# Identity products on TensorE in its waits between the stages of an eight-layer transformer kernel

## The chip, the cores and the metric

The kernel runs on one core of one Trainium2 chip. The metric is the device time in microseconds of one execution. TensorE is called PE here, VectorE DVE, ScalarE ACT and GpSimd POOL.

## What is computed

Tokens x of shape (8, 256, 128) pass four times through an attention and a feed-forward layer, each with a residual and ahead of each a layer norm without gain; a context of shape (8, 64, 128) feeds the attention layers. Cut to the order:

```python
x = x + L0_xattn(layernorm(x), ctx)          # 16 heads, one key/value head
x = x + L0_ffn(layernorm(x))                 # soft mixture: 16 experts, 64 slots each, gelu
x = x + L1_xattn(layernorm(x), ctx)          # similarity w1.q + w2.c + w3.(q*c), both directions
x = x + L1_ffn(layernorm(x))                 # 64 experts of width 88, top 8, two shared experts
x = x + L2_xattn(layernorm(x), ctx, ctx)
x = x + L2_ffn(layernorm(x))                 # 8 experts (4x128, 4x256), top 2, relu squared
x = x + L3_xattn(ctx, ctx, layernorm(x))
x = x + L3_ffn(layernorm(x))                 # quantised linear, depthwise convolution, silu, linear
```

The routed experts are computed for all tokens, and a token's weight for an expert (zero where it isn't chosen) multiplies the hidden values.

## The kernel before

The 2048 tokens lie in SBUF as 16 tiles of 128; four tiles make a group g (512 columns when transposed), so each layer has four groups. The layers are numbered 0 to 7 in the code (L, two to each pair above). Each engine has its own program, written out by hand, and they meet only by semaphores; an engine's order of work is the order of its lines.

At the border of two layers the same chain runs for each group: the residual is added on DVE (L1233, or L1391, L1433, L1581 and L1642 behind attention), DVE takes mean and variance (L1189, L1192, L1195), POOL the inverse root (L586), and DVE (L1202) or POOL (L591, L592) makes xn. On PE ln_transpose waits for xn (semaphore ln_xn), and transposes four tiles with the identity (L1729); ACT copies the result to SBUF (L762). ln_transposes(L) does the four groups one after the other; layers 3 and 5 have router products between them.

Behind the expert stage of layer 1 (eo, comb_ready) PE multiplies the context with w_sim2, then waits for cw_done (DVE L1398), transposes layer 2's groups and makes similarities. The waits for sim_sub and e1_norm stand ahead of transposes at L1968 and L1972. Layer 3 begins with its router products and the shared experts (shared_gate_up); then PE waits for sil_s, and chunk_group1(0, True) begins the 44 chunks of the routed experts with a wait for the first weights' low part (wgu_lo, POOL L624), which POOL makes only when the routing weights are ready (DVE L1480). Inside it, routing_rows transposes them and spreads them over the partitions. After the experts come layer 4 (project, scores, and an attention output per tile t that waits for x_done), layer 5 (router, combine_rows2, 12 chunks of experts), layer 6 in the form of layer 4, and layer 7.

mm is the helper at L1710 that issues every product that isn't a transpose; transposes have their own lines. A product of fp32 operands shows as two MATMUL instructions in the trace, one of fp32r operands as one. psum is eight banks of 512 columns; bank(k) is one of them.

Of the kernel before, what the change touches and what calls it, by code (L numbers as in the profile page):

```python
# [12 lines left out]
P = 128  # L13
# [34 lines left out]
def build_program(nc, A, out):  # L48
    with ExitStack() as ctx:
        def sb(name, shape, dt=F32):  # L50
            return ctx.enter_context(nc.sbuf_tensor(name, shape, dt))
# [4 lines left out]
        psum = ctx.enter_context(nc.psum_tensor("psum", [P, 8, 512], F32))  # L56
# [6 lines left out]
        ident = sb("ident", [P, P])  # L63
# [76 lines left out]
        def bank(k):  # L140
            return psum[:, k, :]
# [1566 lines left out]
        def _(pe):  # L1708
            def mm(dst, lhsT, rhs, start=True, stop=True):
                return pe.matmul(dst, lhsT=lhsT, rhs=rhs, start=start, stop=stop)  # L1710

            def product(dst, w, x):
# [2 lines left out]
                mm(dst, w(0), x(1), False, False)  # L1715
                return mm(dst, w(1), x(0), False, True)

            def ln_transpose(L, g):
                pe.wait_ge(ln_xn, NG * L + g + 1)
                into = LN_BANKS[L][g] if L in LN_BANKS else 6 + g % 2  # L1720
                if g >= 2 and L not in LN_BANKS:
                    pe.wait_ge(ln_xnT, NG * L + g - 1)
                if g == 1 and L == 1:
                    pe.wait_ge(x_done, NT)
                if L == 3 and g == 3:
                    pe.wait_ge(ln_xnT, NG * L + 1)
                    pe.wait_ge(xh_lo, 1 + E0)
                for j in range(4):
                    last = pe.transpose(psum[:, into, P * j:P * j + P], xn[:, 4 * g + j, :], ident[:, :])  # L1729
                last.then_inc(ln_tp, 1)  # L1730

            def ln_transposes(L):
                for g in range(NG):
                    ln_transpose(L, g)
# [15 lines left out]
            for t in range(NT + 3):  # L1750
# [18 lines left out]
                if t >= 3:  # L1769
                    u = t - 3  # L1770
# [4 lines left out]
                if 1 <= t <= NT:  # L1775
                    u = t - 1
# [5 lines left out]
                if t >= 3:  # L1782
                    u = t - 3
# [4 lines left out]
                if 2 <= t <= NT + 1:  # L1788
                    u = t - 2
# [11 lines left out]
            for g in range(NG - 1):  # L1801
                ln_transpose(1, g)
# [55 lines left out]
            pe.wait_ge(se_T, 2)  # L1858
            logits_slots(0)
            ln_transpose(1, NG - 1)  # L1860
            logits_slots(1)
            for q in range(4 * B + 2):
# [76 lines left out]
            for q in range(B // 2):  # L1939
                last = mm(psum[:, 0, q:q + 1], ctxT[:, P * q:P * q + P], cols[:, COL["w_sim2"]:COL["w_sim2"] + 1])  # L1940
            last.then_inc(simT_mm, 1)

            def sim_T(q):

                pe.wait_ge(simT_sb, q + 2)
                for a in range(TB):
                    last = pe.transpose(psum[:, 4 + q // 2, 256 * (q % 2) + P * a:256 * (q % 2) + P * a + P],
                                        simT[:, q, P * a:P * a + P], ident[:, :])
                if q % 2:
                    last.then_inc(sim_mm, 1)  # L1950

            pe.wait_ge(cw_done, 1)
            for q in range(B // 2 + 2):
# [9 lines left out]
                if q >= 2:  # L1963
                    sim_T(q - 2)

            pe.wait_ge(sim_sub, 2)
            for a in range(TB):
                last = pe.transpose(psum[0:B, 7, P * a:P * a + P], mx1b[:, B * a:B * a + B], ident[:, :])  # L1968
            last.then_inc(bt_tp, 1)
            for u in range(NT // 2):  # L1970
                pe.wait_ge(e1_norm, u // 4 + 1)
                last = pe.transpose(psum[:, 2 + u // 4, P * (u % 4):P * (u % 4) + P],  # L1972
                                    e1n[:, 2 * u:2 * u + 2, :].rearrange("p r j -> p (r j)"), ident[:, :])
                if u % 4 == 3:
                    last.then_inc(aT_tp, 1)
# [57 lines left out]
            def gate_up1(n, s, slot):  # L2033

                q, k = s % 4, s % 2
                if later(n, 2):
                    pe.wait_ge(nl_done, n - 1)
                product(bank(k), lambda h: wgu[:, slot, h, 0:P], lambda h: norm_half(q, h)).then_inc(gate_ready, 1)
                if later(n, 2):
                    pe.wait_ge(hid_done, n - 1)  # L2040
                product(bank(2 + k), lambda h: wgu[:, slot, h, P:2 * P], lambda h: norm_half(q, h)).then_inc(up_ready, 1)

            def down1(n, s, slot, start=False, stop=False):
                pe.wait_ge(hh_lo, n + 1)
                acc = bank(4 + s % 4)
                mm(acc, wdn[:, slot, 0, :], hh[:, s % 4, 0, :], start, False)
                mm(acc, wdn[:, slot, 0, :], hh[:, s % 4, 1, :], False, False)
                mm(acc, wdn[:, slot, 1, :], hh[:, s % 4, 0, :], False, stop).then_inc(down_done, 1)

            def routing_rows():  # L2050

                pe.wait_ge(rw_done, 1)
                for q in range(NG):
                    for j in range(4):
                        last = pe.transpose(psum[:, 4 + q, P * j:P * j + P], rw[:, 4 * q + j].rearrange("p k e -> p (k e)"), ident[:, :])
                    last.then_inc(rw_tp, 1)
                for k in range(NG * RG):
                    e, q = k // NG, k % NG
                    if e >= 1:
                        pe.wait_ge(rb_sb[q % 2], 2 * e + q // 2 - 1)  # L2060
                    else:
                        pe.wait_ge(rwr_lo, q + 1)
                    mm(bank(4 + q), selr[:, e, :], rwr[:, 512 * q:512 * q + 512]).then_inc(rb_mm, 1)
                for q in range(NG):
                    pe.wait_ge(rb_sb[q % 2], 2 * RG + q // 2 - 1)

            def chunk_group1(j, first=False):

                for s in range(4 * RG):
                    slot = s // 4 % 2  # L2070
                    if s % 4 == 0:
                        pe.wait_ge(wgu_lo, j * RG + (s // 4 + 1) + STEPS0)
                    gate_up1(j * (4 * RG) + s, s, slot)
                    if first and s < 3:
                        if s == 1:
                            routing_rows()
                        continue
                    if s % 4 == 3:
                        pe.wait_ge(wdn_lo, j * RG + (s // 4 + 1))
                    down1(j * (4 * RG) + (s - 3), s - 3, slot if s % 4 == 3 else 1 - slot, first and s < 7)  # L2080
# [4 lines left out]
                shared_gate_up(m)  # L2085
            pe.wait_ge(rl_sig, 2)
            pe.wait_ge(sil_s, 2 * NG)
            chunk_group1(0, True)
            with pe.Fori(1, NC1 // RG) as j:
                chunk_group1(j)  # L2090
# [43 lines left out]
            for t in range(NT):  # L2134
                b = t // TB
                pe.wait_ge(e2_sb, max(t // 4 + 1, 2 if t == 3 else 1))
                if t >= 4:
                    pe.wait_ge(x_done, 4 * NT + t - 3)
                if t == 0:
                    pe.wait_ge(v2_sb, 1)  # L2140
                mm(psum[:, t % 4, 0:D], e2T[0:C, P * t:P * t + P], v2[0:C, b, :]).then_inc(av2_ready, 1)
# [35 lines left out]
                mm(bank(4 + q), wdn[:, c % 2, 0, :], hh[:, n % 4, 1, :], False, c == NC2 - 1).then_inc(down_done, 1)  # L2177

            def combine_rows2():
                pe.wait_ge(rw_done, 2)  # L2180
                for q in range(2):
                    half = bank(4 + q).bitcast(BF16)
                    for j in range(8):
                        last = pe.transpose(half[0:3 * E2, P * j:P * j + P], cpk[:, 8 * q + j, :], identb[:, :])
                    last.then_inc(rw_tp, 1)
                pe.wait_ge(pool_made, 2)
                pe.wait_ge(rw_sb, 2)
                for k in range(2 * NG):
                    e, q = k // NG, k % NG
                    if e:  # L2190
                        pe.wait_ge(rb_sb[q % 2], 2 * RG + q // 2 + 1)
                    mm(bank(4 + q), sel2[0:3 * E2, e, :], cT[0:3 * E2, 512 * q:512 * q + 512]).then_inc(rb_mm, 1)
                for q in range(2):
                    pe.wait_ge(rb_sb[q], 2 * RG + 4)

            for n in range(UNITS2 + 3):
                if n < UNITS2:
                    up2(n)
                if n == 3:
                    combine_rows2()  # L2200
                if n >= 3:
                    down2(n - 3)
# [12 lines left out]
            for b in range(B):  # L2215
                g = b // 2
# [163 lines left out]
```

## Time and profile before

| | |
|---|---|
| median of 3 runs | 1088.63 us (1088.04 to 1097.9) |
| the profiled execution | 1088.47 us |
| its span, first to last instruction | 1086.3 us |
| mean granted clock of TensorE | 0.919 |
| PE busy | 950.2 us (87%) |
| DVE busy | 728.9 us (67%) |
| ACT busy | 557.3 us (51%) |
| POOL busy | 502.8 us (46%) |

The 2.2 us between execution and span lie around the first and the last instruction. The granted clock is the share of 2.4 GHz that PE was given: it is 1.00 or 0.50 at any time, and a number between is a mean over both.

### The profile page before, as it was taken

Reading aid. Unit: us, or ns where it says so; the run is one execution under the profiler, and the core shown is the slowest. Engines: PE = TensorE matmul, PEld = TensorE weight load, DVE = VectorE, ACT = ScalarE, POOL = GpSimd, SP = SyncE. Lnnn points to the kernel's source line nnn. Section 1 sums busy time; section 2 is a strip of 40 time slices with the busy share of each in tenths; the row PEclk is TensorE's granted clock in tenths of the full one; section 3 lists DMA queues with packets and bytes.
Section 4 is the critical chain, followed back from the end, with each engine's and each line's share of the span. In section 5 each row is a group of like instructions: output and inputs, shape, how many; then the busy total and the mean of one; then the engine's idle time right before and its main releaser. Section 6 shows DMA issues by size and latency. Waiting matters only on the chain.

```text
span 1086.3 us, 15531 instructions
## 1 busy us (share of the span) xinstructions
PE 950.2 (87%) x4485; PEld 716.7 (66%) x4485; DVE 728.9 (67%) x1602; ACT 557.3 (51%) x1077; POOL 502.8 (46%) x512
## 2 busy tenths in 40 slices
PE   5699799999999686999999999999996779966564
PEld 3577566656669482688888888888864746635353
DVE  7677455546554478666666666666756888867796
ACT  2355466666550324666666666666641334433684
POOL 6012222223321310377777777777753449973200
PEclk9899899999999898999999999999997679988566
DMA  5000000003210000000000000000001000000001
GB/s 174 1 1 2 1 1 1 1 1 97 72 53 2 25 1 0 21 25 28 22 24 27 22 22 28 22 22 28 19 0 59 1 0 1 1 1 1 1 10 29
DMA packets 26964, 22.90 MB, mean 21 GB/s; under 512 B 3403, under 2 KB 23971, under 8 KB 26787
## 3 DMA queue, kind: packets, MB, share of 16 engines
q1 hardware_dynamic: 26915, 22.30, 6.9%
q8 instruction: 24, 0.39, 0.2%
q14 instruction: 25, 0.20, 0.1%
HBM read 21.24 MB, written 1.05 MB: 21 GB/s over the span
## 4 chain that ended last, share of the span: by engine, by line
PE 73%; DVE 17%; POOL 3%; ACT 3%; issue 2%; DMA 0%; SPq 0%; DVEq 0%; ACTq 0%
PE psum L1710 66%; DVE stats L1189 1%; PE psum L1832 1%; PE psum L1840 1%; PE psum L1780 1%; POOL rstd L586 1%; DVE xn L1202 1%; DVE arena L1265 1%; POOL hh L666 1%; PE psum L1729 1%; DVE mv L1192 1%; PE psum L1903 1%; DVE arena L1660 1%; DVE arena L1661 1%; DVE arena L1667 1%
## 5 line engine op out<-in xcount | busy, mean ns | idle before, releaser
L1710 PE MATMUL psum<-xall,wgu 128*128 128x512 f32 x1424 | 390.8, 408 | 16.8 <-POOL wgu L624 9.8
L1710 PEld LDWEIGHTS psum<-xall,wgu 128*128 128x128 f32 x1424 | 272.7, 194 | 88.2 <-issue 25.6
L632 POOL TENSOR_TENSOR hh<-arena,hh 128x512 fp32r<-128x512 f32 x176 | 227.9, 1295 | 81.4 <-ACT hh L762 80.1
L1710 PE MATMUL psum<-hh,wdn 128*128 128x512 f32 x672 | 197.0, 399 | 5.4 <-ACT hh L762 3.5
L1499 DVE TENSOR_TENSOR psum<-psum,arena 128x512 f32<-128x512 f32 x176 | 123.0, 699 | 98.4 <-PE psum L1710 92.1
L985 ACT ACTIVATE arena<-psum 128x512 f32<-128x512 f32 x176 | 105.3, 598 | 131.5 <-PE psum L1710 131.4
L762 ACT ACTIVATE hh<-arena 128x512 fp32r<-128x512 f32 x224 | 140.3, 626 | 46.5 <-DVE arena L1627 43.4
L1710 PEld LDWEIGHTS psum<-hh,wdn 128*128 128x128 f32 x672 | 126.5, 189 | 45.9 <-POOL hh L666 16.1
L1504 DVE TENSOR_TENSOR arena<-psum,arena 128x512 f32<-128x512 f32 x176 | 121.6, 691 | 7.6 <-DVE psum L1499 1.7
L1710 PE MATMUL psum<-arena 128*128 128x18 f32 (+7 forms) x776 | 122.0, 317 | 5.3 <-DVE X L1581 2.6
L762 ACT ACTIVATE arena<-psum 128x1024 f32<-128x1024 f32 (+9 forms) x118 | 79.7, 687 | 90.4 <-PE psum L1710 30.1
L1710 PEld LDWEIGHTS psum<-arena 128*128 128x128 f32 (+3 forms) x776 | 95.0, 193 | 18.8 <-issue 14.8
L586 POOL TENSOR_TENSOR rstd<-veps,neghalf 128x4 f32<-128x4 f32 x24 | 24.2, 1012 | 110.2 <-DVE veps L1195 109.9
L721 POOL TENSOR_TENSOR arena<-arena 128x512 f32<-128x512 f32 x32 | 33.3, 1039 | 83.6 <-DVE arena L1317 83.5
L666 POOL TENSOR_TENSOR hh<-arena,hh 128x512 fp32r<-128x512 f32 x48 | 61.9, 1293 | 20.4 <-ACT hh L762 19.7
L624 POOL TENSOR_TENSOR wgu<-egu,wgu 128x256 fp32r<-128x256 f32 x44 | 32.8, 745 | 41.9 <-DVE arena L1480 28.2
L604 POOL TENSOR_TENSOR wgu<-egu,wgu 128x256 fp32r<-128x256 f32 x32 | 23.9, 749 | 56.6 <-ACT wgu L762 56.6
L1729 PE MATMUL psum<-ident,xn 128*128 128x128 f32 x112 | 26.0, 390 | 24.5 <-POOL xn L592 14.2
L1362 DVE SCALAR_TENSOR_TENSOR arena<-psum,ebias,arena 128x512 f32<-128x512 f32 x32 | 24.0, 751 | 32.7 <-PE psum L1710 31.6
L830 ACT ACTIVATE arena<-psum,arena 128x256 f32<-128x256 f32 x64 | 29.7, 469 | 24.9 <-DVE arena L1310 24.2
L1619 DVE SCALAR_TENSOR_TENSOR arena<-psum,arena 128x512 f32<-128x512 f32 x48 | 33.1, 691 | 13.6 <-PE psum L1710 12.9
L762 ACT ACTIVATE xnT<-psum 128x512 f32<-128x512 f32 x24 | 14.3, 598 | 53.4 <-PE psum L1729 53.3
(281 smaller groups left out, 1383.1 us busy)
## 6 DMA issues: line engine op xcount, KB each, us to landing
egu<-in_w SPq DMA_DIRECT2D x44, 128.0 KB, 2.0
egu<-in_egu SPq DMA_DIRECT2D x16, 256.0 KB, 2.7
edn<-in_w SPq DMA_DIRECT2D x44, 64.0 KB, 1.8
edn<-in_edn SPq DMA_DIRECT2D x16, 128.0 KB, 2.1
arena<-in_w SPq DMA_DIRECT2D x1, 1536.0 KB, 7.1
X<-in_x SPq DMA_DIRECT2D x4, 256.0 KB, 4.0
out<-X SPq DMA_DIRECT2D x4, 256.0 KB, 2.3
arena<-in_ctxTd SPq DMA_DIRECT2D x1, 512.0 KB, 5.2
```

What stands on the lines that cost most here:

```text
L586: pool.tensor_tensor(rstd[:, s], veps[:, s], neghalf[:, s], ALU.pow).then_inc(ln_rstd, 1)
L624: pool.tensor_tensor(wgu[:, slot, 1, :], w1gu(slot), wgu[:, slot, 0, :].bitcast(F32), ALU.subtract).then_inc(wgu_lo, 1)
L632: pool.tensor_tensor(hh[:, s % 4, 1, :], h1[:, s % 2, :], hh[:, s % 4, 0, :].bitcast(F32), ALU.subtract).then_inc(hh_lo, 1)
L666: pool.tensor_tensor(hh[:, n % 4, 1, :], h2[:, n % 2, :], hh[:, n % 4, 0, :].bitcast(F32), ALU.subtract).then_inc(hh_lo, 1)
L721: pool.tensor_tensor(qb[:, k % 2], qb[:, k % 2], wide(recB[:, k % 2].unsqueeze(2), 2, N), ALU.mult)\
L762: return act.activation(dst, src, ACT.Copy)
L985: act.activation(sil[:, k, :], bank(k), ACT.Silu).then_inc(nl_done, 1)
L1499: dve.tensor_tensor(bank(2 + k), bank(2 + k), sil[:, k, :], ALU.mult).then_inc(prod_done, 1)
L1504: dve.tensor_tensor(h1[:, k, :], bank(2 + k), rwb[:, s // 4, own], ALU.mult).then_inc(hid_done, 1)
L1619: dve.scalar_tensor_tensor(v2w[:, n % 3, :], bank(q), 0.0, cB[:, 0 if n < 4 * NG else 1, 512 * q:512 * q + 512], ALU.max, ALU.mult)\
L1710: return pe.matmul(dst, lhsT=lhsT, rhs=rhs, start=start, stop=stop)
L1729: last = pe.transpose(psum[:, into, P * j:P * j + P], xn[:, 4 * g + j, :], ident[:, :])
```

## The change

A helper keep_warm(k, n) multiplies the 128x128 identity by itself n times into the first 128 columns of bank k. Nobody reads the result. It is called ahead of waits of PE: in ln_transpose for some groups of layers 3, 4 and 6, and at seven written-out places (two of them in loops). It waits for nothing and signals nothing.

```diff
+            def keep_warm(k, n):
+
+                for _ in range(n):
+                    mm(psum[:, k, 0:P], ident[:, :], ident[:, :])
+
+            WARM_LN = {(3, 3): (4, 5), (4, 0): (5, 16), (4, 1): (5, 9), (4, 2): (5, 5), (4, 3): (5, 2),
+                       (6, 0): (5, 16), (6, 1): (5, 8), (6, 2): (5, 4)}
+
             def ln_transpose(L, g):
+                if (L, g) in WARM_LN:
+                    keep_warm(*WARM_LN[L, g])
                 pe.wait_ge(ln_xn, NG * L + g + 1)
@@ -1939,6 +1949,7 @@
             last.then_inc(simT_mm, 1)
+            keep_warm(1, 14)
@@ -1963,11 +1974,14 @@
+            keep_warm(1, 5)
             pe.wait_ge(sim_sub, 2)
@@
             for u in range(NT // 2):
+                if u % 4 == 0:
+                    keep_warm(1, 5)
                 pe.wait_ge(e1_norm, u // 4 + 1)
@@ -2085,6 +2099,7 @@
             pe.wait_ge(sil_s, 2 * NG)
+            keep_warm(7, 36)
             chunk_group1(0, True)
@@ -2135,6 +2150,8 @@
                 if t >= 4:
+                    if t % 4 == 0:
+                        keep_warm(6, 5)
                     pe.wait_ge(x_done, 4 * NT + t - 3)
@@ -2177,12 +2194,14 @@
             def combine_rows2():
+                keep_warm(6, 3)
                 pe.wait_ge(rw_done, 2)
@@
                     last.then_inc(rw_tp, 1)
+                keep_warm(6, 6)
                 pe.wait_ge(pool_made, 2)
                 pe.wait_ge(rw_sb, 2)
```

## Rows read from the trace of the kernel before

**Rows 1.** The page: granted clock in 40 slices; the last chain by engine.

```profile
PEclk9899899999999898999999999999997679988566
...
PE 73%; DVE 17%; POOL 3%; ACT 3%; issue 2%; DMA 0%; SPq 0%; DVEq 0%; ACTq 0%
```

**Rows 2.** Stretches of PE: from:to, length, busy (instructions), granted clock, DMA share, GB/s.

```profile
361.00:364.00 3.00, 2.97 (x10) 0.50 0.01 3
...
374.40:381.20 6.80, 5.70 (x26) 0.50 0.01 2
...
434.20:439.20 5.00, 4.97 (x12) 0.50 0.16 43
...
828.90:835.10 6.20, 6.20 (x9) 0.50 0.01 3
845.50:848.80 3.30, 2.35 (x17) 1.00 0.00 0
...
858.90:865.60 6.70, 6.70 (x32) 0.50 0.00 0
...
972.00:975.00 3.00, 3.00 (x5) 0.50 0.00 0
...
387.20:393.40 6.20, 6.20 (x58) 1.00 0.00 0
```

**Rows 3.** PE timeline: start, length, what, [idle before <- releaser]; similarity stage, and L2101.

```profile
361.03 1.97 PE L1729 MATMUL psum<-ident,xn 128*128 128x128 f32 x8 [3.88 <-DVE arena L1398]
362.90 1.73 PE L1710 MATMUL psum<-xnT,arena 128*128 128x512 f32 x2
...
364.90 1.02 PE L1710 MATMUL psum<-xnT,arena 128*128 128x512 f32 x2
...
814.58 1.91 PE L2101 MATMUL psum<-ident,arena 128*128 128x128 f32 x16
```

**Rows 4.** PE timeline, the three waits for sim_sub and e1_norm.

```profile
372.07 0.38 PE L1968 MATMUL psum<-ident,arena 128*8 128x128 f32 x2 [1.58 <-DVE arena L1407]
373.62 0.66 PE L1972 MATMUL psum<-ident,arena 128*128 128x128 f32 x4 [1.17 <-DVE arena L1413]
375.50 1.11 PE L1972 MATMUL psum<-ident,arena 128*128 128x128 f32 x4 [1.22 <-DVE arena L1413]
```

**Rows 5.** PE timeline, layer 3's last transposes and the first routed experts.

```profile
406.42 0.66 PE L1729 MATMUL psum<-ident,xn 128*128 128x128 f32 x4 [1.47 <-DVE xn L1202]
...
434.23 5.31 PE L1710 MATMUL psum<-xall,wgu 128*128 128x512 f32 x12 [9.81 <-POOL wgu L624]
```

**Rows 6.** ACT timeline, the last copy of the shared experts.

```profile
424.95 0.58 ACT L762 ACTIVATE arena<-psum 88x512 f32<-88x512 f32 x1
```

**Rows 7.** PE timeline, layer 4's transposes.

```profile
820.87 0.66 PE L1729 MATMUL psum<-ident,xn 128*128 128x128 f32 x4 [4.39 <-POOL xn L592]
824.08 1.11 PE L1729 MATMUL psum<-ident,xn 128*128 128x128 f32 x4 [2.56 <-POOL xn L592]
826.36 2.34 PE L1729 MATMUL psum<-ident,xn 128*128 128x128 f32 x8 [1.17 <-DVE xn L1202]
```

**Rows 8.** The chain that ended last, in order of time: start, length, piece.

```profile
828.85 13.52 PE psum L1710 x60
```

**Rows 9.** PE timeline, layer 6's first and last transposes.

```profile
964.72 0.98 PE L1729 MATMUL psum<-ident,xn 128*128 128x128 f32 x4 [4.39 <-POOL xn L592]
...
970.03 2.14 PE L1729 MATMUL psum<-ident,xn 128*128 128x128 f32 x8 [1.00 <-DVE xn L1202]
```

**Rows 10.** Layer 4's attention output and combine_rows2: PE timeline, and one chain piece.

```profile
849.16 2.04 PE L1710 MATMUL psum<-arena 64*128 64x128 f32 x8 [1.32 <-DVE X L1581]
...
852.13 1.04 DVE X L1581 x4
...
872.88 1.06 PE L2184 MATMUL psum<-identb,arena 128*24 128x128 bf16 x16 [0.52 <-DVE arena L1606]
875.60 3.06 PE L1710 MATMUL psum<-arena 24*128 24x512 bf16 x8 [1.65 <-ACT arena L762]
```

## Prediction

> **What bounds the kernel now.** I read the page first. Its chain of the work that ended last is 73% TensorE and 17% VectorE, so a microsecond of PE counts only where PE is the end of the chain; the long expert stage in the middle is such a place, but nothing is edited inside it. The line of granted clock on the same page falls below 9 tenths in places, nearly all of them between the expert stages, where layers of normalisation, attention and routing alternate [rows 1]. Second, I asked for busy time and granted clock in short stretches. The reader is to see three kinds there: stretches in which PE works without a pause at half clock (361 to 364, 374.4 to 381.2, 434.2 to 439.2, 828.9 to 835.1, 858.9 to 865.6, 972 to 975 us), a stretch at full clock in which fp32 products of 128 columns run (387.2 to 393.4), and one at full clock with PE busy 2.35 of 3.30 us, all of it small work on 64 rows, after which the clock is at half all the same (845.5 to 848.8) [rows 2]. Third, I read PE's timeline around each of these for the wait ahead of it. The pattern is the same in most: PE waits one to ten microseconds, the clock goes to 1.2 GHz, and the work after the wait pays for it. The time is bounded there by PE's work at 1.2 GHz, where the chain goes through PE, and by the VectorE and GpSimd pieces that make PE wait.
>
> **What the change adds.** Nothing is removed or moved. Counting calls: 5 before group 3 of layer 3's transposes, 16+9+5+2 = 32 in layer 4's, 16+8+4 = 28 in layer 6's, 14 after the first w_sim2 products, 5 before the wait for sim_sub, 2x5 at the e1_norm waits, 36 before the first chunk of experts, 3x5 in the layer-2 attention output, 3+6 in combine_rows2: 154 products. They have no semaphore, no DMA, and add nothing to another engine's queue; whatever stands behind them on PE waits for them.
>
> **Price of one.** The operands are fp32, 128x128 by 128 columns, as in the qv projection: 58 instructions took 6.20 us at full clock [rows 2], two instructions a product, so 0.214 us; I take 0.22. At half clock I take twice that, 0.43: a 512-column fp32 product (two instructions) took 1.02 us at full clock and 1.73 where most of it was at half [rows 3], and columns are what both are made of. All 154 are 34 us of PE at full clock, 66 at half. They are free only if they fit in the waits, so I go place by place: what they fill, then what the clock gives back.
>
> **a) Into the sim stage.** PE waits 3.88 us for DVE L1398 [rows 3]. 14 x 0.22 = 3.1 us fits. Behind it, at 361 to 364 us, the clock is at half. The chain takes 8 transposes and the first product of w_sim (1.97 then, after overlap, about 1.64 us). At full clock the first four transposes take 0.5 (16 took 1.91), the xnT copy 0.6 and the product 0.86, which ends at 361.03+0.5+0.6+0.1+0.86 = 363.1 in place of 364.6 [rows 3]: 1.5 us. Three fills of 5 (1.1 us each) stand in waits of 1.58, 1.17 and 1.22 us [rows 4]: they fit, the last two by 0.1. Behind them PE works 5.70 of 6.80 us at half clock [rows 2], and it is the chain there. Halving would give 2.85; the products on 64 rows shorten less, and the copies in between stay, so 2.4 us.
>
> **b) Into the first experts.** Before group 3 of layer 3 PE waits 1.47 us, the 5 fit [rows 5]; what follows on the chain is routing on DVE, so I take 0.2. The 36 start when ACT has copied the last shared up-projection, at 424.95+0.58 = 425.5 [rows 6], and take 36 x 0.22 = 7.9 us, to 433.4; PE is released at 434.23 after a 9.81 us wait for POOL L624 [rows 5]. They fit with 0.8 us to spare. The 12 products behind it take 4.97 us at half clock [rows 2] and about 12 x 0.22 = 2.6 at full. The routing transposes come next; their input is made by DVE L1480, the piece that releases L624 too, so they are ready by then. So 2.4 us.
>
> **c) Into layers 4 and 6.** The waits are 4.39, 2.56 and 1.17 us [rows 7] against 16, 9 and 5 products = 3.5, 2.0 and 1.1: all fit; the 2 before group 3 (0.44) fit where group 2's transposes shrink from 1.2 to 0.5. From 828.85 the chain is 13.52 us of PE in one piece [rows 8], of which 6.20 is at half clock [rows 2]: 3.1 us. Layer 6 has the same form: a first wait of 4.39 and a last of 1.00 [rows 9] against 3.5 and 0.9, and one between them for the 8 (1.8). Behind them two groups of transposes (2.14) and 3.0 us of projection run at half clock [rows 2, 9]; 1.5 from the projection and 0.3 from the last transposes, 1.8 us.
>
> **d) Attention output and router of layer 5.** 5 before t = 4, 8 and 12. The wait at t = 8 is 1.32 us (t = 12 has the same), at t = 4 there is none, so PE is 1.1 us late for tokens 4 to 7 and, 1.1 late and filling 1.1, about 0.9 late for 8; PE makes token 8 from 849.16 on and DVE L1581 takes it at 852.13 [rows 10], which hides it: cost 0, at most 1.1 if it doesn't. What could be gained is at 858.9 to 865.6, 6.70 us of PE at half clock on the chain: up to 3.4. Nothing is added between 854 and 866, though, and PE's work there is transposes and products with 8 columns; 845.5 to 848.8 shows that the clock went down after PE was 71% busy with other small work [rows 2]. I take 0, and keep 3.4 as the other end.
>
> **e) combine_rows2.** 3 products stand in a wait of 0.52 us [rows 10], after a cold stretch, and the rows don't fix whether the clock is back by then: 0.66 at full, 1.28 at half, so 0.1 to 0.8 us is lost. 6 (1.3 us) fit in 1.65. The 8 products for the weight rows then take at full clock about 2.2 in place of 3.06 (the second four wait for copies of 0.6 to 0.7): 0.85 gained. Net 0.6, ends -0.3 and 0.9. The wait of PE after it, for the first hidden values, is not filled, so the cold start of the second experts stays.
>
> **Sum.** 1.5 + 2.4 + 0.2 + 2.4 + 3.1 + 1.8 + 0 + 0.6 = 12.0 us. The profiled execution took 1088.47 us (span 1086.3), the median is 1088.63: no correction. 1088.5 - 12.0 = 1076.5. Lowest end of the costs: router gained too, -3.4. Highest: late PE in d, e at its bad end, a half of a) behind DVE and ACT: +1.1 +0.9 +2.0, 1080.5. After about 990 us nothing is edited; clock changes there need not fall at the same places, for which I allow 2 us either way.
>
> Here a page and the rows differ. At 814.58 us 16 fp32 transposes took 1.91 us at full clock, 0.12 each, and at 970 us 8 took 2.14 at half, 0.27 each [rows 3, 9]. The Trainium skill (TensorE: Matmul & The Clock Gate, Part 4: PE-mode transpose) says that the full clock does not engage for transposes; by that the part of the gain that is transposes, some 1.5 us, would be missing, and the time 1078.0. The trace decides against it.
>
> **Rivals.** *The router is warm too.* The 15 products of d keep 2.4 GHz through 866 us. For it: they fill the gaps at 849 and 852 us. Against it: 4 us of light work with nothing added. 1076.5 - 3.4 = 1073.1.
> *The clock goes down between short fills.* In layers 4 and 6 the pauses stay cut up (fill, wait, four transposes), and 845.5 to 848.8 shows a fall with PE mostly busy. Then c) gives nothing: 1076.5 + 4.9 = 1081.4. Against it: the fills are full-size products, not small ones. The Trainium skill (TensorE: Matmul & The Clock Gate, A second HAM failure mode: psum-queue depth-cycling) describes a PE that idles briefly between groups and whose clock swings for it; by that rule it is this rival that comes, and the trace bears it out only in the one place named.
> *Gains off the chain.* PE is faster, but ACT copies and DVE end the stages; half of a), b) and c) is kept: 1088.5 - 6 = 1082.5. Against it: the 13.52 us piece without any other engine [rows 8].
> *Slower: the fills start cold.* If the clock is at half when the first fill of a place starts, it outlasts its wait: 16 x 0.43 = 6.9 in 4.39, 36 x 0.43 = 15.5 in 8.7, 14 x 0.43 = 6.0 in 3.88. Over all places that is 6.8 + 2.1 + 2.1 + 5.5 + 4.3 us and 2.5 for d and e, 23, and no gain: 1111. It decides from the point where a fill takes over 0.27 us a product (4.39/16). The rows show full clock before each of these waits.
> *Nothing happens:* the clock does not answer to these products: 1088.5.
>
> **How the numbers follow.** Forecast 0.55, router 0.12, clock falls in layers 4 and 6 0.16, off the chain 0.10, slower 0.04, nothing 0.03. About 1% (10.9 us, below 1077.7) is what a measurement of this kernel can tell from no change. The forecast lies 1.2 us below that line and is sure to about 2 us, so about three quarters of it, 0.42, count as faster; with the router 0.12 and a rest of 0.05 from small surprises, 0.59. Slower 0.04, within 1% 0.37. The range goes from under the router case, 1071.5, to the off-chain case, 1082.5.
>
> **What would show it.** In the changed profile the granted clock should be 1.00 at the places of a), b) and c) shifted by what was gained before them; the waits for L1398, L624 and L592 should be cut to under 1 us; the 12 products after L624 should take 2.6 us, and the piece from the wsum product on about 10.4 in place of 13.52. The clock should still be at half around the router of layer 5 and in the last attention and the last layer, where nothing is added. Wrong would be: a wait of PE turned into a wait of DVE or ACT for the identity products, the clock at half after a fill, or a stage that ends at the same distance although PE is faster.

## The result

| | before | after |
|---|---|---|
| median of 13 runs | 1089.85 us | 1082.62 us |
| lowest, highest | 1088.04, 1097.9 | 1074.96, 1085.69 |
| ratio to before | | 0.991 (95%: 0.9888 to 0.9932) |
| profiled execution | 1088.47 us | 1083.58 us |
| its span, mean granted clock | 1086.3 us, 0.919 | 1081.8 us, 0.946 |

The change is worth 0.7 to 1.1%. The median lies 6 us above the point forecast and 0.1 us above the range's upper end of 1082.5. Taken as shares of the before beside each, the measured 0.9% is inside the range, which went from 0.6% to 1.6% of 1088.5. It is on the other side of the 1% line from where more than half of the chance lay. Ten runs lie between 1081 and 1086 us, three at 1075 to 1077. Cold is short for half clock here, warm for full clock.

The waits were filled as counted. This is PE's timeline of after (start, length, what, idle before and its releaser); compare [rows 3], [rows 5], [rows 7] and [rows 8]:

```profile
357.98 3.37 PE L1710 MATMUL psum<-ident 128*128 128x128 f32 x28
362.01 1.09 PE L1739 MATMUL psum<-ident,xn 128*128 128x128 f32 x8 [0.66 <-DVE arena L1398]
...
422.04 8.28 PE L1710 MATMUL psum<-ident 128*128 128x128 f32 x72 [1.26 <-ACT arena L762]
431.27 3.06 PE L1710 MATMUL psum<-xall,wgu 128*128 128x512 f32 x12 [0.96 <-POOL wgu L624]
...
817.81 3.74 PE L1710 MATMUL psum<-ident 128*128 128x128 f32 x32
822.36 0.65 PE L1739 MATMUL psum<-ident,xn 128*128 128x128 f32 x4 [0.82 <-POOL xn L592]
...
830.55 1.10 PE L1710 MATMUL psum<-ctxT,wk 128*128 128x512 f32 x2
831.49 3.60 PE L1710 MATMUL psum<-xnT,wq 128*128 128x512 f32 x8
```

14 products (28 instructions) leave 0.66 us of a wait of 3.88, the 36 leave 0.96 of 9.81, the 16 leave 0.82 of 4.39. Behind them the 12 products take 3.06 us in place of 5.31, and eight transposes 1.09 in place of 1.97.

And this is what was not foreseen. PE's timeline of after, from the last routed experts of layer 3 to the transposes ahead of layer 4:

```profile
797.76 0.84 PE L1710 MATMUL psum<-hh,wdn 128*128 128x512 f32 x3
800.34 12.43 PE L1710 MATMUL psum<-arena,sdT 88*128 88x512 f32 x16 [1.74 <-DVE arena L1508]
811.78 4.44 PE L1710 MATMUL psum<-hh,wdn 128*128 128x512 f32 x9
816.06 1.91 PE L2116 MATMUL psum<-ident,arena 128*128 128x128 f32 x16
```

Busy time and granted clock of PE in stretches of after (from:to, length, busy (instructions), clock, DMA share, GB/s):

```profile
362.00:365.00 3.00, 2.68 (x15) 1.00 0.01 3
375.40:381.60 6.20, 6.18 (x51) 1.00 0.00 0
431.30:434.20 2.90, 2.90 (x13) 1.00 0.22 68
...
830.50:836.50 6.00, 6.00 (x26) 1.00 0.00 0
...
969.30:973.50 4.20, 4.20 (x12) 1.00 0.00 0
...
802.00:815.60 13.60, 13.60 (x21) 0.50 0.00 0
...
817.80:829.90 12.10, 9.94 (x82) 1.00 0.36 131
```

The first five are stretches that stood at 0.50 in [rows 2], and 817.8 to 829.9 is the stage of layer 4's fills and transposes: all at full clock. The one from 802.0 us is at half, and was at full clock in the profile of before. No line of it was edited: it is the shared down-projection (sdT, 88 rows) and the last down-projections of the experts. In the profile of before the same 16 instructions took 7.13 us and the 9 after them 2.61:

```profile
805.55 7.13 PE L1710 MATMUL psum<-arena,sdT 88*128 88x512 f32 x16 [1.74 <-DVE arena L1508]
812.12 2.61 PE L1710 MATMUL psum<-hh,wdn 128*128 128x512 f32 x9
```

Laying the timelines side by side at the first instruction of each stage gives the account. "+fill" is experiment 1 below. Each entry is the length from one start to the next in before, less that in the other kernel; positive is won:

| from, to (start in before) | forecast | after | +fill |
|---|---|---|---|
| begin to w_sim2 products (356.20) | 0 | -0.97 | -0.17 |
| a) to first qv product (385.98) | 3.9 | 3.68 | 3.67 |
| b) to first weight-row product (441.40) | 2.6 | 2.51 | 2.51 |
| routed experts, to sdT (805.55) | 0 | -0.01 | -0.03 |
| sdT, to transposes (814.58) | 0 | **-6.69** | -0.01 |
| c) layer 4, to its e2 transposes (842.90) | 3.1 | 3.12 | 3.12 |
| d) to experts of layer 5 (866.90) | 0 | 0.01 | 0.19 |
| e) to first down product (882.18) | 0.6 | 0.69 | 0.68 |
| experts of layer 5, to output transposes (958.42) | 0 | -0.04 | -0.75 |
| c) layer 6, to output projection (990.42) | 1.8 | 2.00 | 1.98 |
| layer 7, to the end (1086.28) | 0 | 0.13 | 0.07 |
| sum | 12.0 | 4.43 | 11.26 |

### The profile page after: what moved, and what is told of

It reads as the page before. It is cut to its first block and busy times, and to the rows that moved or that the text cites. A ratio compares the mean times of both kernels' runs of the same rounds, so it can differ in the third digit from the quotient of the medians.

```text
span 1081.8 us, 16144 instructions
## 1 busy us (share of the span) xinstructions
PE 968.8 (90%) x4793; PEld 739.0 (68%) x4793; DVE 729.4 (67%) x1602; ACT 557.2 (52%) x1077; POOL 503.0 (46%) x512
## 3 DMA queue, kind: packets, MB, share of 16 engines
HBM read 21.24 MB, written 1.05 MB: 21 GB/s over the span
## 5 line engine op out<-in xcount | busy, mean ns | idle before, releaser
L1710 PEld LDWEIGHTS psum<-xall,wgu 128*128 128x128 f32 x1424 | 269.7, 191 | 78.2 <-issue 15.0
L1504 DVE TENSOR_TENSOR arena<-psum,arena 128x512 f32<-128x512 f32 x176 | 121.7, 691 | 7.7 <-DVE psum L1499 1.7
L1710 PE MATMUL psum<-arena 128*128 128x18 f32 (+7 forms) x776 | 117.0, 306 | 1.2 <-DVE X L1703 0.8
L1710 PEld LDWEIGHTS psum<-arena 128*128 128x128 f32 (+3 forms) x776 | 91.4, 187 | 14.2 <-issue 10.2
L624 POOL TENSOR_TENSOR wgu<-egu,wgu 128x256 fp32r<-128x256 f32 x44 | 32.8, 745 | 39.4 <-DVE arena L1480 28.0
L595 POOL TENSOR_TENSOR rtmp<-veps,neghalf 128x4 f32<-128x4 f32 x4 | 4.0, 1006 | 78.1 <-DVE veps L1195 78.1
```

The costliest lines, as they stand in the source:

```text
L624: pool.tensor_tensor(wgu[:, slot, 1, :], w1gu(slot), wgu[:, slot, 0, :].bitcast(F32), ALU.subtract).then_inc(wgu_lo, 1)
L1504: dve.tensor_tensor(h1[:, k, :], bank(2 + k), rwb[:, s // 4, own], ALU.mult).then_inc(hid_done, 1)
```

## The experiments

Theory A: the wait of 1.74 us ahead of sdT is one where the clock falls in some executions of either kernel and not in others. (Why is a guess that no run tests: that a wait and the light work around it meet the clock's own steps, which would lie differently in each execution.) Theory B: the fall at sdT is caused by the fills, as by what ran before it. Further rivals stand with each run.

**1. One more fill, ahead of sdT.** The wait for hid_done (DVE L1504, the hidden values of the experts before) is new too; it keeps the fill from bank 0 until the experts' products there have been used.

```diff
+            pe.wait_ge(hid_done, UNITS1 - 1)
+            keep_warm(0, 7)
             pe.wait_ge(hs_done, 2 * NG)
             for g in range(NG):
```

> The changed kernel with one more fill: 7 identity products into bank 0 in PE's 1.74 us wait for DVE L1508, ahead of the shared down-projection (sdT). Theory A (the clock falls there in some executions, since the work and the wait ahead of it meet the clock's steps differently each time, and the 88-row products run 6.7 us longer at half clock): no execution shows half clock in that stretch, the piece from the first sdT product to the transposes of layer 4 is 9.0 us and not 15.7, and the times close up around 1076.5, about 6 us below the changed kernel's median. Theory B (the fall there has another cause, as that the experts before it ran longer at full clock): the stretch stays at 15.7 us in most executions and the median stays near 1082.5. Theory C (no lasting effect: what is won there is lost to a wait of layer 4): 9.0 us in the stretch but a median over 1080.

Measured: median 1076.8 us, five of six runs from 1076.2 to 1077.1 (the sixth took 1180.2 us at a mean granted clock of 0.804; no profile shows why, and the ratio leaves it out), ratio to before 0.9869 (0.9832 to 0.9905). PE's timeline of this kernel at the place:

```profile
797.66 1.72 PE L1710 MATMUL psum<-ident 128*128 128x128 f32 x14
799.57 7.13 PE L1710 MATMUL psum<-arena,sdT 88*128 88x512 f32 x16 [0.18 <-DVE arena L1508]
806.14 2.63 PE L1710 MATMUL psum<-hh,wdn 128*128 128x512 f32 x9
```

The products take 7.13 us again, the median is 5.8 us below the changed kernel's, and but for that sixth run the spread of 11 us is gone. The expectation's B and C fall, and what A says of the times and the stretch holds; its reason for the falls (the clock's steps) is not shown by this.

**2. The kernel before with that fill alone** (the same edit, and keep_warm itself).

> The kernel before with nothing but the 7 products ahead of the shared down-projection. Theory A: the executions at 1094 to 1098 (5 of 13 of the kernel before) are those in which the clock fell there; they vanish, and all times lie within 2 us of 1088.5. Theory B (the high times have another cause): they stay in about one execution in three.

Measured: median 1088.31 us, 12 runs from 1086.8 to 1089.9, while 29 runs of the kernel before beside it went from 1086.9 to 1097.4, 14 of them above 1090.5 and seven above 1093.8. Both kinds vanish. Experiment 9 shows the place for the highest; of the seven between 1090.5 and 1093.8 there is no profile, so what this fill does to them is open.

**3. Fills as long, but eight columns wide**

```diff
-                    mm(psum[:, k, 0:P], ident[:, :], ident[:, :])
+                    mm(psum[:, k, 0:8], ident[:, :], ident[:, 0:8])
```

> The changed kernel with the same 154 fills, but each product has 8 columns in place of 128; the rows of before give 0.115 us for an instruction so narrow at full clock, so PE is kept as long. Theory A (the columns streamed keep the clock, not that PE has an instruction): the clock is at half again behind the waits, 12 us of gain are gone, time 1088 to 1095. Rival (any instruction keeps the clock): 1076 to 1083 as the changed kernel.

Measured: median 1101.91 us (1094.3 to 1103.6), ratio 1.0095 (1.0068 to 1.0121): slower than before, by more than was expected. The ten runs fall into two kinds, three from 1094.3 to 1095.8 and seven from 1100.3 to 1103.6. The profile is of the fastest, 1094.3, and in it sdT to the transposes takes 9.04 us, so the clock did not fall there. This kernel has no fill at sdT, and six of the seven higher runs have a mean clock lower by 0.005 to 0.008 than the lower three, as most of after's higher runs have against its lower ones (0.945 to 0.948 against 0.951). So the higher kind is probably the fall at sdT again; no profile of one shows it. PE's timeline, and stretches of it, ahead of the routed experts of layer 3:

```profile
425.13 12.45 PE L1710 MATMUL psum<-ident 128*128 128x8 f32 x72 [1.26 <-ACT arena L762]
437.43 5.17 PE L1710 MATMUL psum<-xall,wgu 128*128 128x512 f32 x12
```

```profile
425.10:428.40 3.30, 3.27 (x30) 1.00 0.00 0
428.60:437.40 8.80, 8.80 (x43) 0.50 0.08 24
437.50:442.00 4.50, 4.50 (x12) 0.50 0.00 0
```

PE has an instruction all the time, and the clock falls nevertheless in the middle of the fill. From there each fill takes 0.2 us an instruction and not 0.11, so the 36 take 12.45 us in place of 8.28 and outlast their wait: from the first shared product to the 12 products it is 28.96 us (408.47 to 437.43) where before had 25.17 (409.06 to 434.23), and the 12 products are cold as before. These 3.8 us are the largest part of the 6.3 by which the span of this profile is over before's. So the narrow fills themselves cost about 6 us, and the median's 12 is not theirs alone. This is the slower rival of the prediction, by another cause than a cold start: a fill that loses the clock takes about twice its time from there on.

**4. Layers 4 and 6 alone** (the kernel before, keep_warm, and WARM_LN without its entry for layer 3). The expectation names the 7 products too, but this kernel doesn't have them; in its profile PE waits 1.74 us for L1508, as in before, and the clock holds:

```profile
804.52 7.13 PE L1710 MATMUL psum<-arena,sdT 88*128 88x512 f32 x16 [1.74 <-DVE arena L1508]
```

> The kernel before with the fills of layers 4 and 6 alone (32 and 28 products), and the 7 ahead of the shared down-projection. Theory A: each place gives its own gain, 3.1 us in layer 4 and 2.0 in layer 6, so 5.1 us below the kernel before with the 7 alone (about 1083.4). Rival (the gains hang together: without the fills of the stages before, the clock's steps fall elsewhere and one of them is lost): under 3.5 us.

Measured: median 1083.61 us, 4.7 below experiment 2; in its profile layer 4 won 3.14 us between wsum and the e2 transposes, layer 6 1.98. The gains add up place by place in the profile. Seven of the ten runs lie from 1081.5 to 1083.9; the other three took 1088.0, 1088.1 and 1091.7 at lower mean clocks. They are not profiled; with no fill at sdT, a fall there is possible. No fill of this kernel stands ahead of sdT, and three high runs in ten are about the rate of before (21 of 66, below).

**5. Without the 36**

```diff
-            keep_warm(7, 36)
```

> The changed kernel with the 7 products ahead of the shared down-projection, without the 36 ahead of the first routed experts. Theory: these 36 do nothing but keep the clock for the 12 products behind them (3.1 us then, 5.3 without), and every other place keeps its gain: 2.3 us above the 1076.8 of the kernel that has them, so 1079.1. Rival (the long wait can't be paid for by its first 12 products alone, more of the stage behind is cold): over 1081.

Measured: median 1077.98 us of four runs (1077.3 to 1082.6), 1.2 above experiment 1. In the profiles the way from the first shared product to the first weight-row product is 32.38 us without them, 29.81 with them (experiment 1): 2.6 us by the place, where 2.3 were expected. The medians, of four and six runs, are too few to tell 1.2 from 2.3. Against the rival: the stages behind keep their lengths. The profiled execution is the one of 1082.6; 3.2 us of what it has over experiment 1 arose ahead of the w_sim2 products (359.57 against 356.37), in stages that are the same in both.

**6. Without the 15 in the attention output**

```diff
-                    if t % 4 == 0:
-                        keep_warm(6, 5)
```

> The changed kernel with the 7 products, without the 15 in layer 4's attention output. My prediction had put them at nothing won and nothing lost: 1076.8, within 0.5 us. Rival (they keep the clock longer into the router of layer 5 in a part of the executions): 0.5 to 2 us slower without them.

Measured: median 1077.8 us of four runs (1075.7 to 1079.3), 1.0 above experiment 1, within its scatter. By the profiles the way from wsum to the experts of layer 5 is 34.91 us without them and 34.72 with them, against 38.05 in before, where layer 4's cold products are in it. They win 0.2 us at most in what was profiled. Whether they win more in some executions stays open. The profiled execution is the highest of the four, and it too was 3.1 us late at the w_sim2 products (359.44).

**7. Every fill twice as long**

```diff
-                for _ in range(n):
+                for _ in range(2 * n):
```

> The changed kernel with the 7 products, and every fill twice as long. By the waits of the trace a doubled fill of 0.43 us a product outlasts its wait by 2.1 us (14), 2.4 (three of 5), 0.7 (layer 3), 6.7 (36), 5 (layer 4), 4.3 (layer 6), 2 (attention output), 1.5 (combine_rows2), 1.2 (the 7): 26 us, so about 1103, at full clock throughout. Rival (what follows on PE has slack of its own): under 1090.

Measured: median 1096.88 us (1094.4 to 1100.8), 20.1 above experiment 1, at the same mean clock (0.951 in its profile, 0.950 there). So most of what a fill does beyond its wait is paid, and my 26 us were too many by nearly a quarter. Against experiment 1, the profile lost 6.9 us at the 36 (6.7 expected), 4.4 in the similarity stage (4.5), 0.6 in layer 3 (0.7), 1.1 at sdT (1.2), 2.0 in combine_rows2 (1.5), but only 3.5 in layer 4 (5) and 2.9 in layer 6 (4.3). From layer 4's e2 transposes to the experts of layer 5, where 2 were to be lost, it won 1.5: with the doubled fills the granted clock was 1.00 there from 850 to 870 us. PE's timeline:

```profile
426.15 16.32 PE L1710 MATMUL psum<-ident 128*128 128x128 f32 x144 [1.26 <-ACT arena L762]
442.22 3.00 PE L1710 MATMUL psum<-xall,wgu 128*128 128x512 f32 x12
...
823.13 7.31 PE L1710 MATMUL psum<-ident 128*128 128x128 f32 x64
830.28 0.60 PE L1739 MATMUL psum<-ident,xn 128*128 128x128 f32 x4
```

16.32 us for 72 products is 0.227 each; 7.31 us for 32 sets the transposes 8.90 us behind the output transposes' start (821.38), where experiment 1 has 6.30.

**8. More fills.** Experiment 1, with the fills that the expectation lists; the parts that count:

```diff
+                    if u == 0:
+                        keep_warm(7, 40)
                     pe.wait_ge(exp_done, u + 1)
...
-                       (6, 0): (5, 16), (6, 1): (5, 8), (6, 2): (5, 4)}
+                       (6, 0): (5, 16), (6, 1): (5, 8), (6, 2): (5, 4), (5, 1): (5, 4), (5, 2): (5, 8), (1, 3): (4, 9)}
...
+            keep_warm(4, 10)
             expert_pair(0)
...
-                pe.wait_ge(xq_done, g + 1)
                 if g >= 2:
                     pe.wait_ge(xq_lo, g - 1)
+                keep_warm(0 if g < 2 else 2 + g % 2, (8, 20, 12, 16)[g])
+                pe.wait_ge(xq_done, g + 1)
...
-                pe.wait_ge(gi_done, q + 1)
                 if q:
                     pe.wait_ge(gi_sb, q)
+                keep_warm(6, (14, 3, 9, 9, 12, 2, 9, 11)[q])
+                pe.wait_ge(gi_done, q + 1)
```

> The changed kernel with the 7 products and fills in the waits that it leaves open: 40 ahead of the first transposes of attention 0, 9 ahead of group 3 in layer 1, 10 ahead of the first experts of layer 1, 4 and 8 ahead of groups 1 and 2 in layer 5, 14 behind combine_rows2, and in layers 6 and 7 5 and 18 in the output projection, 8, 20, 12 and 16 ahead of the token transposes, 2 to 14 ahead of each transpose of integers. Theory: where PE is on the chain behind them it gains: about 2 at the start, 1.5 in layer 1, up to 3 in the router of layer 5, 1 behind combine_rows2, and 2 to 4 in layer 7, where PE is a small part of the chain: 1065 to 1069. Rival (layer 7 is bound by DVE and ACT, and the fills there delay what they should speed up): 1070 or more.

Measured: median 1068.17 us, six runs from 1065.9 to 1069.0, ratio 0.9781 (0.9749 to 0.9812), mean clock 0.986. It is faster than both kernels. Against before its profile wins 2.12 us in the router of layer 5 (row d, 0.01 to 0.19 in after and experiment 1) and 4.6 behind the first product of layer 7.

**9 and 10. The kernel before, two more executions**

> The kernel before, unchanged, for the profile of one more execution. Theory A: the time goes by the places at which the clock is at half. If this execution lies at 1094 or more, its piece from the first shared down-projection to the transposes of layer 4 takes about 15.7 us (as in the changed kernel's profile) and not 9.0; if it lies under 1090, that piece takes 9.0. Rival: a high time with 9.0 us there.

> The same as the run before it: one more execution of the kernel before, with the same two expectations (15.7 us in the piece where the time is 1094 or more, 9.0 where it is under 1090).

Measured: 1096.67 and 1086.89 us, one of each kind. PE's timeline at sdT in the first of them:

```profile
804.78 0.84 PE L1710 MATMUL psum<-hh,wdn 128*128 128x512 f32 x3
807.36 12.90 PE L1710 MATMUL psum<-arena,sdT 88*128 88x512 f32 x16 [1.74 <-DVE arena L1508]
```

and in the second:

```profile
804.30 7.13 PE L1710 MATMUL psum<-arena,sdT 88*128 88x512 f32 x16 [1.74 <-DVE arena L1508]
810.87 2.61 PE L1710 MATMUL psum<-hh,wdn 128*128 128x512 f32 x9
```

The wait is 1.74 us in both, and the experts' stage ahead of it took 364.2 and 364.1 us. From the first sdT product to the transposes it is 15.75 us in the one and 9.02 in the other, 6.7 of the 9.4 us between their spans. The slow one is also 3.95 us late at the w_sim2 products (358.57 against 354.62) and wins 1.3 back elsewhere. This settles that the fall happens without the change too.

Part of the 3.95 us is a second place of the same kind, ahead of layer 1's first experts, where PE waits 2.72 us for DVE L1355. In before the clock stays full and the 18 products behind it take 4.67 us; in experiment 1 it falls and they take 5.95, with the same program up to there:

```profile
245.21 5.95 PE L1710 MATMUL psum<-xall,wgu 128*128 128x512 f32 x18 [2.72 <-DVE xall L1355]
```

Of the profiles without a fill there, 1, 5, 6, 7 and 9 have the fall, and before, after, 2, 3, 4 and 10 don't. Over all profiles the start of the w_sim2 products ranges from 354.6 to 359.6 us, in stages that the change doesn't edit.

**11. More fills without those of layer 7 and the output projection ahead of it**

> The kernel with more fills, without those in layer 6's output projection and in layer 7. In the trace of the one with them the last 70 us (layer 7 and the output projection ahead of it) took 4.6 us less than in the kernel before, after the first router of layer 7 at 1012 us. Theory (layer 7's gain is its fills' doing): 4.5 us slower than with them, about 1072.7. Rival (it comes with an earlier start or other steps of the clock): under 1070.

Measured: median 1070.65 us (1070.3 to 1071.1), ratio 0.9818 (0.9789 to 0.9846), 2.5 slower than experiment 8. In the profiles layer 7 (from its first product to the end) is 73.2 us here, 69.6 with its fills and 74.2 in before: 3.6 by the place. The expected 4.5 were too high, as 1.0 of the 4.6 us came without these fills; the rival's under 1070 isn't met. Layer 7 pays little: 125 products there win 3.6 us, and the 23 in the output projection none (21.7 us from its start to layer 7's first product in all three). That PE holds only a part of the chain there is the likely reason; no run tests it.

## Why the forecast stood where it did

*The working of a) to e).* It held nearly everywhere, by the table: 3.68 for 3.9, 2.51 for 2.6, 3.12 for 3.1, 0.69 for 0.6, 2.00 for 1.8, together 12.0 for 12.0. The price of a fill was right (0.22 forecast; 8.28 us for 36 is 0.23), the fits too, down to the 36 (0.96 us left, 0.8 forecast). Inside the terms some errors cancel. In a) the start of the stage won 1.1 us in place of 1.5, the part behind the three fills of 5 won 2.6 in place of 2.4. In b) the 12 expert products took 3.06 us, not 2.6: the price of an identity product had been put on products of another shape, and 2.26 us were won in place of 2.4. Of the 0.2 us before the 36 nothing shows up to the shared products, which start 0.2 us after DVE's xall L1226; the 0.26 won behind them is little more than the 0.09 to 0.17 in profiles without layer 3's fill (2, 4 and 10).

*The router.* The 0 was right, but not for the reason given. That the clock would be at half around the router was one of the prediction's signs, and it came only in part. In before PE is cold from 849 us on, through the attention output and the whole router. In after the 15 fills kept it warm about 8 us longer, and it fell in the wait ahead of the third group:

```profile
851.05 1.16 PE L1710 MATMUL psum<-arena 64*128 64x128 f32 x8
852.14 0.66 PE L1739 MATMUL psum<-ident,xn 128*128 128x128 f32 x4
853.85 0.66 PE L1739 MATMUL psum<-ident,xn 128*128 128x128 f32 x4 [1.05 <-POOL xn L592]
...
857.20 1.12 PE L1739 MATMUL psum<-ident,xn 128*128 128x128 f32 x4 [1.90 <-POOL xn L592]
```

The attention output (1.16 us for 8 instructions in place of 2.04) and two groups of transposes were warm, and still the stage took as long (0.01 us won): PE then waited for POOL's xn, 1.05 and 1.90 us. What PE holds on the chain seems to lie behind the third group, which was still cold. With 12 products more, at groups 1 and 2, the clock held to 852.5 us, almost the end of the router, and the stage won 2.12 us (experiment 8); with the doubled fills it won 1.72 (experiment 7). The 3.4 us kept as the other end were not out of reach, only not with these fills.

*The step that failed* is a term that the sum put at nothing: the places ahead of 990 us that aren't edited. Behind it stands "The pattern is the same in most". I looked at stretches that were cold in one profile and took all others as warm for good. One sentence allowed 2 us for clock changes behind 990 us; none was allowed for before. In truth the wait at L1508 (1.74 us, in the profile of before and filled nowhere) is a place where the clock falls or doesn't: in the kernel before 5 of 13 runs lie above 1094, in the changed one 10 of 13 above 1081. The fall costs 6.7 us. Four profiles show it directly (after and run 9 have the fall, before and run 10 don't); for the runs without a profile it is inferred from the time and the mean clock, which in after is 0.951 in the three low runs and 0.940 to 0.948 in the ten others. So the changed kernel's median is that of its executions with the fall, and before's is of its executions without it. The 1076.5 us forecast is the time of the three runs at 1075 to 1077, and of experiment 1. The fall is more frequent after the change: 10 of 13 against 5 of 13. Over 66 runs of before, 21 lie above 1093.8, and 12 more between 1090.2 and 1093.5 are of a kind that no profile shows. If only the highest count, the difference is hardly chance. In the kernels with fills ahead of sdT and none at it, ten of 13 (after) and seven of ten (experiment 3) are high, with fills only behind it three of ten (experiment 4). So fills ahead of it seem to favour the fall, perhaps by the time at which they bring PE to the wait. That is inferred from times, not from profiles, so a part of theory B stays open.

*The high run of before* (1097.9 was in the table of times) was there to be asked about. Two of the three runs agreed to 0.6 us and the third took 9 us more, which was read past.

*Luck.* The range's upper end, 1082.5, was set by the rival "gains off the chain", and the measured 1082.6 lies next to it and to the 1081.4 of "the clock goes down between short fills". Neither is what happened: the gains of a), b) and c) came whole. That the median lies at the end of the range comes from a place that the prediction didn't price.

*The rivals.* The clock fell between no short fills in layer 4 (817.8 to 829.9 us at full clock), and it was full behind those of layer 6 (969.3 to 973.5). The Trainium skill (TensorE: Matmul & The Clock Gate, A second HAM failure mode: psum-queue depth-cycling) tells of a PE whose clock swings with brief idling; these stages don't show it. Nor did the gains of a), b) and c) vanish behind ACT and DVE. The Trainium skill (TensorE: Matmul & The Clock Gate, Part 4: PE-mode transpose) says that the full clock doesn't engage for transposes, and the trace contradicts it again: the eight of layer 2 took 1.09 us in after and 1.97 in before, and each group of four in layers 4 and 6 took 0.65 or 0.66, where 824.08 and 964.72 in before had 1.11 and 0.98 ([rows 7], [rows 9]).

## What to carry to other kernels

Where TensorE sets the pace behind a wait, full-width products that nobody reads, as long as the wait and no longer, shorten the work behind it that would run cold: here by 12 us at the edited places, 11.5 in the medians of experiments 2 and 1, and about 20 us of 1088 with the further waits of experiment 8. Make them wide (eight columns didn't hold the clock and turned the gain into a loss), and size them at the full-clock price a little under the wait. Fill the waits that fall in some executions only, too, and not only those that were cold in the one profile: look at the spread of the times first, and where it has two humps, find the place whose length differs between two profiles.

## What the runs showed that was not expected

- From 802.0 to 815.6 us of after PE was busy for 13.60 of 13.60 us and stayed at half clock. To about 812 us this was the shared down-projection on 88 rows, then expert products on 128. In before the 12 expert products on 128 rows were cold for 434.2 to 439.2 us ([rows 2]), and the 16 transposes behind them took 1.91 us, as at full clock. So a fall ahead of sdT is far dearer (6.7 us) than one ahead of expert products (2.3 at L624, 1.3 at L1355). The number of rows and the type (fp32 there, fp32r in the experts) differ both, and no run tells which of them matters.
- With equal program and equal waits the clock falls in one execution and not in the next (experiments 9 and 10), at two places at least: the wait for L1508, and the wait for L1355.
- A fill that is too narrow loses the clock while PE is never idle (425.1 to 437.4 us in experiment 3).
